# Gated cross-attention and ternary FFN on one core: 16-bit split projections, a new order of work, and a whole batch's attention result held in two PSUM banks

## The reference

```python
x = x + tanh(g_xattn) * xattn(layernorm(x), ctx)     # 16 heads of 16 columns, softmax over 128 keys, then @ Wo
x = x + tanh(g_ffn)   * ffn(layernorm(x))            # 256 -> 1024 -> gelu -> 256, ternary weights
# xattn: q = x @ Wq, k = ctx @ Wk, v = ctx @ Wv; softmax(q k^T / 4) v; @ Wo
```

## Time and profile before

| | us |
|---|---|
| median of 3 runs | 1667.67 (1663.63 to 1668.81) |
| profiled execution, its own time | 1664.17 |
| its span | 1662.4 |

### The profile page before, as it was taken

The page is one execution under the profiler, slowest core; times in us unless marked ns, Lnnn a source line. Parts: engine busy times, 40 slices in busy tenths (PEclk is TensorE's granted clock), DMA queues, the critical chain, the costliest instruction groups (busy, mean ns, idle before and its releaser), DMA issues.

```text
span 1662.4 us, 48262 instructions
## 1 busy us (share of the span) xinstructions
PE 1508.0 (91%) x14501; PEld 1007.7 (61%) x14501; DVE 1489.1 (90%) x4379; ACT 939.8 (57%) x1799; POOL 668.8 (40%) x813
## 2 busy tenths in 40 slices
PE   3899999999999999999999999987999999999998
PEld 2566666666666666666666666655666666666665
DVE  7799999999999999999999999987888888888886
ACT  2456666665656666565656566654555555555554
POOL 5354555455555545554555545552111111111111
PEclk9899999999999999999999999996999999999999
DMA  2333333333333333333333333321010110101101
GB/s 78 92 99 85 96 84 88 93 86 97 84 96 83 97 84 94 86 87 95 86 97 83 98 83 95 81 49 55 26 38 25 38 38 25 38 25 38 38 25 51
DMA packets 207471, 117.93 MB, mean 71 GB/s; under 512 B 24912, under 2 KB 207184, under 8 KB 207440
## 3 DMA queue, kind: packets, MB, share of 16 engines
q1 hardware_dynamic: 207440, 117.54, 26.2%
HBM read 32.53 MB, written 16.78 MB: 30 GB/s over the span
## 4 chain that ended last, share of the span: by engine, by line
PE 55%; DVE 26%; issue 13%; ACT 3%; DVEq 2%; ACTq 0%; DMA 0%
PE bank L1069 12%; PE bank L312 9%; PE bank L1098 5%; PE bank L1099 5%; DVE smax L751 5%; PE bank L336 5%; PE bank L319 4%; PE bank L303 4%; DVE rstd L691 3%; DVE xres L796 3%; DVE k L721 3%; PE bank L392 2%; DVE rstd L693 2%; DVE y L1056 2%; DVE rstd L684 2%
## 5 line engine op out<-in xcount | busy, mean ns | idle before, releaser
L924 POOL TENSOR_TENSOR probl<-prob 128x512 f16<-128x512 f32 x512 | 529.2, 1042 | 531.2 <-ACT prob L602 530.3
L602 ACT ACTIVATE prob<-bank,masks 128x512 f32<-128x512 f32 x512 | 345.4, 688 | 138.9 <-PE bank L371 138.9
L751 DVE TENSOR_REDUCE smax<-bank 128x4 f32<-128x512 f32 x512 | 348.2, 681 | 13.5 <-PE bank L336 9.7
L1085 DVE TENSOR_TENSOR hidl<-hid 128x512 f16<-128x512 f32 x256 | 226.0, 883 | 80.5 <-ACT hid L1080 79.7
L1080 ACT ACTIVATE hid<-bank,b_sb 128x512 f32<-128x512 f32 x256 | 176.1, 688 | 211.3 <-PE bank L1069 205.3
L1069 PE MATMUL bank<-y,w1T 128*128 128x512 f16 x1024 | 264.6, 381 | 29.2 <-DVE y L1056 28.0
L1163 POOL TENSOR_TENSOR xres<-xres,b2g 128x1024 f32 (+1 forms) x32 | 75.7, 2366 | 431.4 <-ACT yln L1033 413.5
L1098 PE MATMUL bank<-w2T,hid 128*128 128x256 f16 x1024 | 237.4, 273 | 0.6 <-ACT w2T L1013 0.6
L1099 PE MATMUL bank<-w2T,hidl 128*128 128x256 f16 x1024 | 237.4, 273 | 0.0
L336 PE MATMUL bank<-k_rows,q_rows 64*128 64x128 f16 x2048 | 226.8, 220 | 5.6 <-DMA q_rows<-smaxT 3.4
L371 PE MATMUL bank<-q_rows,k_rows 64*128 64x128 f16 x2048 | 201.7, 219 | 0.8 <-DMA q_rows<-smaxT 0.8
(11 more groups left out here) (92 smaller groups left out, 2555.7 us busy)
## 6 DMA issues: line engine op xcount, KB each, us to landing
q_rows<-q SPq DMA_DIRECT2D x512, 64.0 KB, 2.5
k_rows<-k SPq DMA_DIRECT2D x512, 64.0 KB, 2.5
xres<-in_x_dram SPq DMA_DIRECT2D x64, 256.0 KB, 2.7
out_dram<-ystage SPq DMA_DIRECT2D x32, 512.0 KB, 2.9
ctx_sb<-in_ctx_dram SPq DMA_DIRECT2D x64, 192.0 KB, 3.2
q_rows<-smaxT SPq DMA_DIRECT2D x128, 8.0 KB
w_raw<-in_L_ffn_W_dram SPq DMA_DIRECT2D x2, 1024.0 KB, 7.0
prob<-in_L_xattn_Wq_dram SPq DMA_DIRECT2D x1, 256.0 KB, 4.2
```

Source lines behind the costliest of these rows:

```text
L602: act.activation(prob[u][:], st_bank[u % 2][:], ACT.Exp, bias=0.0, scale=masks[g.parity][:, 2 + b:3 + b]).then_inc(exp_done, 1)
L751: dve.tensor_reduce(smax[:, b, u * UH:(u + 1) * UH], sm_bank[u % 2][:].rearrange("p (h j) -> p h j", h=UH), AX.X, ALU.max).then_inc(max_ta ...
L924: pool.tensor_tensor(probl[u][:], prob[u][:], prob[u][:].bitcast(BF16)[:, 1::2], ALU.subtract).then_inc(prob_split, 1)
```

## The change

- q, k, v and the output projection: each float32 operand becomes a pair of 16-bit ones (weights as 64 times their value in two float16 parts; x and the context as the upper 16 bits of the float32 word, read as bfloat16, and a float16 remainder that POOL writes over the lower 16 bits of the same word). Each product is three matmuls instead of one float32 matmul. Transposes of x and of the context are in 16 bits, eight instead of four, and ACT copies a bank of 1024 float16 values out. POOL gets two new operations a group, `low_x` and `low_ctx`; `low_prob` writes into `prob` itself.
- Layer norm of x: by four batches at once, every second group. DVE only starts it (`seed_x`, four parts placed in `dve_group` by `norm(0)` to `norm(3)`), the Newton steps go to POOL (`root_x`, 14 operations).
- `pv_banks` spans two banks and holds all 16 heads of one batch. `read_weighed` and `normalise` work on 16 heads at once, the sum is written back to PSUM, and the first `weigh` of a batch waits for `norm_done` of the batch before it.
- `transpose_attn`, `copy_attnT`, `project_out` and `add_attention` take both batches of a group at once; DVE has a new operation `low_attn`, whose end frees `tr_bank`.
- A new order on all five engines; k has two buffers, and SP moves q and k apart (`move_q`, `move_k`).
- At the start, ACT and DVE make the split weights (12 operations each) in place of 8 copies on DVE.

The core of the diff:

```diff
+            return pj_bank[:].rearrange("p (b m s) -> p m b s", m=KD, b=2)[:, m]
+
...
                 pe.wait_ge(xT_copied, g.n + 1)
             for k in range(KD):
-                last = pe.matmul(pj_bank[:, m * T:(m + 1) * T], wq_sb[:, k, m * P:(m + 1) * P],
-                                 xlnT[:, k, :], start=(k == 0), stop=(k == KD - 1))
+                for i, (wp, xp) in enumerate(SPLIT):
+                    last = pe.matmul(by_batch(m), wq16[:, wp, k, m * P:(m + 1) * P],
+                                     typed(xT16[:, xp, k, :], xp).rearrange("p (b s) -> p b s", b=2),
+                                     start=(k == 0 and i == 0 and m == 0), stop=(k == KD - 1 and i == 2),
+                                     skip_group_check=True)
             if m == KD - 1:
                 last.then_inc(q_made, 1)
...
             if b == 0 and u == 0:
                 pe.wait_ge(v_masked, g.n + 1)
                 pe.wait_ge(v_split, g.n + 1)
-            if u % 2 == 0 and not (isinstance(n, int) and n == 0):
-
-                pe.wait_ge(norm_read, n * 2 + (half - 1))
+            if u == 0 and not (isinstance(n, int) and n == 0):
+
+                pe.wait_ge(norm_done, n)
             for c in range(UH):
-                o = pv_bank[half][:, (c0 + c) * VC:(c0 + c + 1) * VC]
+                o = pv_banks[:, (u * UH + c) * VP:(u * UH + c) * VP + VC]
                 first = (b * HEADS + u * UH + c) * VW
                 v = v16_all[g.parity][:, first:first + VC]
                 high = prob[u][:].bitcast(BF16)[:, 2 * c * S + 1:2 * (c + 1) * S:2]
+                low = prob[u][:].bitcast(F16)[:, 2 * c * S:2 * (c + 1) * S:2]
                 pe.matmul(o, high, v, start=True, stop=False)
-                last = pe.matmul(o, probl[u][:, c * S:(c + 1) * S], v, start=False, stop=True)
...
+            scores(pe, g, 0, 0, (g, 1, 3))
             if not first:
                 weigh(pe, before, 1, 2)
...
+            if left >= 2:
+
+                pe.wait_ge(v_split, g.n + 1)
...
+                project_q(pe, g2, 0)
+
+            scores(pe, g, 0, 1, (g1, 0, 0) if left >= 1 else None)
             if not first:
                 weigh(pe, before, 1, 3)
+            tr = transpose_max(pe, g, 1, tr)
             if left >= 2:
-
-                pe.wait_ge(v_split, g.n + 1)
-                project_q(pe, g2, 0)
+                project_q(pe, g2, 1)
                 tr = transpose_ctx(pe, g2, tr)
-                project_q(pe, g2, 1)
-
-            scores(pe, g, 0, 2, (g1, 0, 0) if left >= 1 else None)
+
+            scores(pe, g, 0, 2, (g1, 0, 1) if left >= 1 else None)
+
+            scores(pe, g, 0, 3, (g1, 0, 2) if left >= 1 else None)
             weigh(pe, g, 0, 0)
-            tr = transpose_max(pe, g, 1, tr)
-
-            scores(pe, g, 0, 3, (g1, 0, 1) if left >= 1 else None)
             weigh(pe, g, 0, 1)
             if not first:
...
+                tr = transpose_attn(pe, before, tr)
...
         def copy_ctxT(act, g):
             act.wait_ge(ctx_transposed, g.n + 1)
             if not (isinstance(g.half, int) and g.n < 2):
...
+        def seed_x(dve, half, i):
+
...
+            if i == 0:
+                dve.wait_ge(x_in, 16 * (half + 1))
+                for b in range(QB):
+                    last = dve.bn_stats(stats[:, b, :], row_of(half * QB + b))
+            elif i == 1:
+
+                if not (isinstance(half, int) and half == 2):
+                    dve.wait_ge(ln_ready, half)
+                dve.wait_ge(seed_step, past * (SEED_PARTS - 1) + 1)
+                dve.tensor_copy(rstd[:, 2, :], stats[:, :, 1])
+                for b in range(QB):
+                    last = dve.bn_aggr(meanvar[:, b, :], stats[:, b, :])
+            elif i == 2:
+                dve.wait_ge(seed_step, past * (SEED_PARTS - 1) + 2)
+                dve.tensor_scalar(newton[:, 2, :], meanvar[:, :, 1], EPS, -0.5, ALU.add, ALU.mult)
+                last = dve.tensor_scalar(newton[:, 0, :], meanvar[:, :, 1], EPS, None, ALU.add)
+            else:
+                dve.wait_ge(seed_step, past * (SEED_PARTS - 1) + 3)
+                dve.tensor_scalar(newton[:, 1, :].bitcast(I32), newton[:, 0, :].bitcast(I32), -0.5, RSQRT_SEED,
+                                  ALU.mult, ALU.add).then_inc(root_seeded, 1)
+                return
+            last.then_inc(seed_step, 1)
+
+        def root_x(pool, half, i):
...
+
+            y, hv, t, mean = (newton[:, k, :] for k in range(1, 5))
+            past = half - 2
...
+                    pool.tensor_tensor(norm[:, 1, :], norm[:, 0, :], mean, ALU.mult).then_inc(ln_ready, 1)
+                    return
+                if i == ROOT_PARTS - 2:
+
+                    pool.wait_ge(ln_done, QB * half)
+                    last = pool.tensor_tensor(norm[:, 0, :], y, t, ALU.mult)
+                elif i % 4 == 1:
+                    last = pool.tensor_tensor(t, y, y, ALU.mult)
+                elif i % 4 == 2:
+                    last = pool.tensor_tensor(t, t, hv, ALU.mult)
+                elif i % 4 == 3:
+                    last = pool.tensor_tensor(t, t, one5[:], ALU.add)
+                else:
+                    last = pool.tensor_tensor(y, y, t, ALU.mult)
+            last.then_inc(root_step, 1)
+
+        def low_x(pool, g):
+            pool.wait_ge(ln_done, 2 * (g.n + 1))
+            x = xln[:].rearrange("p b d -> p (b d)")
+            pool.tensor_tensor(x.bitcast(F16)[:, 0::2], x, x.bitcast(BF16)[:, 1::2], ALU.subtract).then_inc(x_split, 1)
+
...
+        def low_attn(dve, g):
+            dve.wait_ge(attnT_high, g.n + 1)
+            dve.tensor_tensor(attnT16[:, 1].rearrange("p k t -> p (k t)"), tr_bank[:],
+                              attnT16[:, 0].rearrange("p k t -> p (k t)"), ALU.subtract).then_inc(attnT_split, 1)
...
+        def read_weighed(dve, g, b):
+
+            n = g.batch(b)
+            dve.wait_ge(weighed, (n + 1) * UNITS)
+            dve.reciprocal(rsum[:, b, :], pv[:, :, 2 * HD])
+            dve.tensor_reduce(sums, pv[:, :, 0:2 * HD].rearrange("p h (two d) -> p h d two", two=2), AX.X,
+                              ALU.add).then_inc(sums_taken, 1)
+
+        def normalise(dve, g, b):
+
+            dve.wait_ge(sums_taken, g.batch(b) + 1)
+            if not (isinstance(g.half, int) and g.n == 0):
+
+                dve.wait_ge(attn_transposed, g.n)
+            dve.tensor_tensor(attn[b][:], sums, rsum[:, b, :].unsqueeze(2).to_broadcast([P, HEADS, HD]),
                               ALU.mult).then_inc(norm_done, 1)
...
+                if g.parity == 1 and left >= 6 and i < SEED_PARTS:
+                    seed_x(dve, g.half + 3, i)
...
             take_max(dve, g, 1, 3)
+            norm(0)
             round_max(dve, g, 1)
-            norm(10)
+            norm(1)
             low_max(dve, g, 1)
...
+            norm(2)
+            if left >= 1:
+                take_max(dve, g1, 0, 0)
+            norm(3)
+
             if left >= 2:
                 low_q(dve, g2)
-            norm(12)
-            if left >= 1:
...
             if left >= 1:
                 take_max(dve, g1, 0, 1)
-            read_weighed(dve, g.batch(0), 0, 0)
-            normalise(dve, g.batch(0), 0, 0)
+            norm(4)
+            if not first:
+                read_weighed(dve, before, 1)
+                norm(5)
+                normalise(dve, before, 1)
...
             n = g.batch(b) * UNITS + u
             pool.wait_ge(exp_done, n + 1)
-            pool.tensor_tensor(probl[u][:], prob[u][:], prob[u][:].bitcast(BF16)[:, 1::2],
+            pool.tensor_tensor(prob[u][:].bitcast(F16)[:, 0::2], prob[u][:], prob[u][:].bitcast(BF16)[:, 1::2],
                                ALU.subtract).then_inc(prob_split, 1)
 
```

More of the change, by code:

```diff
@@ L317, in project_v @@
         def project_v(pe, g, b):
-            for k, rows in enumerate((P, C1)):
-                last = pe.matmul(pj_bank[:, b * D:(b + 1) * D], ctxT[g.parity][0:rows, k, b * S:(b + 1) * S],
-                                 wv_sb[0:rows, k, :], start=(k == 0), stop=(k == 1))
+            for k in range(2):
+                for i, (wp, xp) in enumerate(SPLIT):
+                    last = pe.matmul(pj_bank[:, b * D:(b + 1) * D],
+                                     typed(ctxT16[g.parity][:, xp, k, b * S:(b + 1) * S], xp),
+                                     wv16[:, wp, k, :], start=(k == 0 and i == 0 and b == 0),
+                                     stop=(k == 1 and i == 2), skip_group_check=True)
             if b == 1:
@@ L460, in pe_group @@
             before, g1, g2 = g.after(-1), g.after(1), g.after(2)
-            tr = [(maxT_copied, 1)] if first else []
-            scores(pe, g, 0, 0, (g, 1, 2))
+            if first:
+                tr = [(maxT_copied, 1)]
+            elif isinstance(g.half, int) and g.n == 1:
+                tr = [(xT_copied, 4)]
+            else:
+                tr = [(x1_done, g.n - 1)]
+            scores(pe, g, 0, 0, (g, 1, 3))
             if not first:
```

(47 more changed lines are left out.)

506 lines of the change are left out of this document (280 added, 226 removed).

## The result

The changed kernel takes 1866.38 us (median of 4 runs, 1856.54 to 1871.58) against 1667.27 (1663.63 to 1668.81): ratio 1.119, 95% interval 1.114 to 1.124. The forecast was 1754 in a range up to 1860, so it had the sign and named the chain of waits, but it had less than half of the loss.

A forecast was written before the change was run, and what follows sets the result against it. The prediction took a chain of waits between engines to bound each group: 17.05 us plus 1.2 for POOL, 18.25 against 16.84. Over 62 groups that adds 87 us, the start 3: 1664 + 87 + 3 = 1754, range 1600 to 1860.

The forecast's parts named there:

- The clock: Rival: PE at 1.2 GHz behind its 2.3 us hole in every second group, 1.5 us a group more, 1847; chance 0.17.
- the first hole: PE idle ahead of a group's first weigh unit, waiting for DVE's sum and scaling: 2.3 us in every group.
- Engine sums: Work per group: DVE 12.5 us, POOL 12.2, ACT near 10.3; as the rival that these decide, 1485 us, chance 0.06.
- The chain: Waits between engines through one attention group, followed from PE's turn: 17.05 us without POOL's waiting; with it, chance 0.50.
- POOL's 0.7 and 1.1 us: DVE's splitting of the maxima held by POOL: 0.7 us lost at the first pair, up to 1.1 at the second.
- The hole ahead of the output projection: PE idle 1.1 us a group, waiting for ACT's high_v and copy of x.
- POOL on the chain: DVE's SBUF-only operations waiting for POOL: nothing to 1.8 us a group, taken as 1.2.
- Start: First q 10 us later for memsets and weight splitting, 7 back from faster projections: +3 us, between -5 and +12.
- SP: SP's moves of k and the maxima land at 15.3 to 15.9 us, just fitting: no gain, a small risk.
- The shorter chain: Rival: hand-overs 0.05 us shorter each and POOL idle at both pairs, 15.95 us a group, 1612; chance 0.22.

The follow-up runs named there:

- all holes filled: Matmuls with unread results added to the changed kernel at four PE holes, the last ahead of batch 0's transposed maxima and v: 1769.91 us.
- (c): Changed kernel with batch 1 read early, q first, low_attn ahead of the fourth maximum, x's transposes earlier, seed ahead of low_v, POOL's root steps later: 1598.22 us.
- the first kernel with added matmuls: Matmuls with unread results added to the changed kernel ahead of the first weigh unit, odd groups' transposed maxima and the output projection: 1830.56 us.

## Why the prediction was wrong, step by step

- **The clock.** This is the step that failed. The forecast had it as a rival with 0.17, at 1.5 us a group, and at nothing in its own sum, with the one reason "the work behind is dense". Measured by itself it is 96 us, 1.6 a group. The forecast's 1754 and these 96 are 1850; the 16 that are left are what the kernel with all holes filled has over the forecast (1770 against 1754). The density of the work behind a hole was no argument: in the windows the clock falls in that dense work. That the rival's 93 us (1.5 x 62) met the 96 is luck. It counted 2.9 us of work at half clock in every second group, behind the first hole alone; in the trace some 7.4 us of a group are at half clock, about half of whose loss never reaches the time, and the holes ahead of batch 0's transposed maxima and v do it too: filling them, as the last of the four, gave 61 of the 96 us. That float32 matmuls took twice their time at 0.5, which the prediction says by rows 11, does not stand in those rows, but in the trace of before: four of L411 take 1.11 us at 1101.88 and 2.05 at 1108.99. The Trainium skill (TensorE: Matmul & The Clock Gate, HAM oscillation) describes a clock that goes cold in every turn of a loop with a wait for a DMA in it. The trace agrees in that the clock falls again and again and never settles, with 0.80 to 0.84 in each 100 us between 400 and 800, but here the waits are for other engines and no hole of PE in these 400 us is longer than 2.5 us.
- **Engine sums.** DVE 0.67 of 20.5 is 13.8 us a group (12.5 and 1.2 of waiting forecast), POOL 0.586 of it is 12.0 (12.2), ACT 11.0 (10.3). Right to 0.7 us or better, and not the bound.
- **The chain.** Of POOL's 0.7 and 1.1 us the forecast took 0.68, so 0.5 in the first stretch and 0.75 in the second. The three stretches, in us (means over 400 to 800 us; `add_attention` starts about 0.2 into the turn, which is added in the first):

| stretch | forecast | changed kernel | all holes filled |
|---|---|---|---|
| start of the turn to the end of the scaling, even / odd groups | 6.8 / 8.4 | 7.1 / 8.8 | 7.1 / 8.4 |
| from there to the end of `low_k` | 5.3 | 5.9 | 5.35 |
| from there to the next `add_attention`, even / odd | 5.5 | 6.7 / 7.1 | 5.6 / 5.6 |

  So at full clock each stretch of the chain was right to 0.3 us or better, and on the mean of both kinds of groups the 1.9 us that went with the clock lie at 0.2, 0.5 and 1.2 in the three: mostly behind `low_k`, not behind the first hole, where the rival had put them.
- **The hole ahead of the output projection**, 1.1 forecast, is 0.2 on the mean (4.7 us over 19.5 groups). PE at half clock comes late itself, which would hide it; that is argued, not shown, since with the holes filled added matmuls stand just there.
- **POOL on the chain.** 1.2 a group forecast, as a share of 1.8; lost by L909 and L916 1.4 in the changed kernel and 1.2 with the holes filled; worth 0.8 when taken away there.
- **Start.** +3 us forecast; the first exponential starts at 54.44 instead of 50.47, 4 later. The last row of exponentials starts at 1330.31 instead of 1128.57, so 198 of the 204 us between the two profiled executions lie in the attention. (The attention before thus lasted until about 1131 us of the span, not until 1107.)
- **SP** did just fit: no wait of PE for a move stands among the six above.
- **The rivals.** The shorter chain and the engine sums did not occur with this order; with the order mended, (c) shows that a group of 15.9 us was in the same instructions.

## What to carry to other kernels

Where a chain of waits leaves PE a hole of one to two us in every turn of a loop, look at the granted clock of the work behind it, put what it costs into the sum and not among the rivals, and ask of each move what it does to the holes: here a move that shortened the chain by 0.6 us a group at full clock made the kernel 0.6% slower by itself. When a trace shows a full engine replaced by three with gaps, look for work whose inputs are ready but which stands in its engine's order behind a wait: one such move gave 159 us, and mending the order 268. Matmuls added to the holes separate the chain from the clock; what they cost themselves was not measured here.

## What the runs showed of the hardware

- During a hole of 2.5 us on PE (501.8 to 504.3) the granted clock was full; the fall to 1.2 GHz came in the busy work behind it, before 506, and lasted until about 508. Six matmuls of k took 1.49 us there and 0.82 at full clock.
- It also fell behind holes of 1.04 and 0.37 us with 0.23 us of work between them (the first kernel with added matmuls, 514.4 to 516.1).
- Half clock cost less than PE's own loss by it: some 7.4 us of a group were at half clock, in which PE loses at most half, 3.7 us (an estimate from the mean of 0.82), and with the clock full a group was 1.9 us shorter (20.5 to 18.6).
- A DVE operation with all its 16-column operands in SBUF took up to 1.01 us behind POOL's operations of 1.04 us. With an input in PSUM and the output still in SBUF none of 90 took more than 0.18, POOL being just as busy (269.8 us of 400, against 258.9).
